# Copies, evictions, projections and the next layer's first work at other steps, and another deal of the down products, in a two-layer attention and feed-forward kernel

## The reference, cut to what matters

```python
# x: (4, 512, 512) float16
xn = _layernorm(x)
q, k, v = xn @ Wq, xn @ Wk, xn @ Wv          # 32 query heads of 16, 8 key heads of 16
attn = softmax((q @ k.T) / sqrt(16))          # per head, 512 x 512
s = (attn @ v) @ Wo
h = silu(x_gate) * x_up                       # x_gate, x_up = fwht(xn * SU_ug) @ W.T, 2048 wide
g = fwht(h * SU_dp) @ W_down.T                # fwht: a Walsh-Hadamard transform
x = x + s * silu(g)
# layer 1: a gated delta-rule attention and a feed-forward with signs of the weights
```

## Time and profile before

| | us |
|---|---|
| median of 3 runs (lowest, highest) | 1400.39 (1399.33, 1401.78) |
| profiled execution, its own time | 1401.55 |
| its span, first to last instruction | 1399.8 |
| first score group to the last one issued | 47.83 to 720.70 |
| layer 1 begins on TensorE | 769.17 |
| PE busy in the span | 1259.5 (90%) |
| DVE, ACT, POOL busy | 1050.2, 787.6, 524.7 |

### The profile page before, as it was taken

The page is one execution under the profiler, slowest core; times in us unless marked ns, Lnnn a source line. Parts: engine busy times, 40 slices in busy tenths (PEclk is TensorE's granted clock), DMA queues, the critical chain, the costliest instruction groups (busy, mean ns, idle before and its releaser), DMA issues. The chain is left out here.

```text
span 1399.8 us, 23475 instructions
## 1 busy us (share of the span) xinstructions
PE 1259.5 (90%) x8738; PEld 643.5 (46%) x8738; DVE 1050.2 (75%) x1823; ACT 787.6 (56%) x1306; POOL 524.7 (37%) x434
## 2 busy tenths in 40 slices
PE   5777977988798897889959999999999999999998
PEld 2332333333333333333324545865477555855475
DVE  6678875778677786778883986868956976968845
ACT  4775765667676685667836752355433652355431
POOL 3589852012211221012301573328431573328431
PEclk9999999999999999999989999999999999999999
DMA  6655643676567765786777024010131024001121
GB/s 238 199 138 95 110 84 72 108 155 136 104 112 156 141 118 96 137 158 119 127 208 283 22 58 90 10 38 27 44 81 38 9 58 91 17 31 40 42 40 46
DMA packets 346561, 135.59 MB, mean 97 GB/s; under 512 B 312176, under 2 KB 333392, under 8 KB 343888
## 3 DMA queue, kind: packets, MB, share of 16 engines
q1 hardware_dynamic: 334032, 132.52, 42.4%
q10 hardware_dynamic: 12416, 1.57, 1.0%
HBM read 44.87 MB, written 17.87 MB: 45 GB/s over the span
## 5 line engine op out<-in xcount | busy, mean ns | idle before, releaser
L1165 PE MATMUL bank<-rows,both 128*128 128x512 f16 x1024 | 250.2, 391 | 38.8 <-DVE th L657 22.4
L944 ACT ACTIVATE probs<-vpair,top_n 128x512 f16<-128x512 f32 x256 | 170.5, 687 | 141.3 <-DVE top_n L638 141.2
L638 DVE TENSOR_REDUCE top_n<-vpair 128x1 f32<-128x512 f32 x256 | 169.3, 682 | 64.5 <-PE bank L1134 64.0
L1179 PE MATMUL bank<-dn,h 128*128 128x512 f16 x768 | 182.6, 386 | 0.0
L1165 PEld LDWEIGHTS bank<-rows,both 128*128 128x128 f16 x1024 | 95.9, 100 | 176.5 <-DVE th L657 36.6
L944 ACT ACTIVATE probs<-bank,top_n 128x512 f16<-128x512 f32 x256 | 164.4, 687 | 0.0
L638 DVE TENSOR_REDUCE top_n<-bank 128x1 f32<-128x512 f32 x256 | 163.3, 678 | 0.0
L454 POOL TENSOR_TENSOR h<-th,h 128x512 f16<-128x512 f32 x61 | 70.5, 1155 | 225.0 <-ACT h L913 225.0
L2246 PE MATMUL bank<-rows,both 128*128 128x512 f16 x512 | 117.3, 380 | 0.0
L1179 PEld LDWEIGHTS bank<-dn,h 128*128 128x128 f16 x768 | 71.3, 99 | 93.7 <-issue 17.8
L2262 PE MATMUL bank<-both,hid 128*128 128x512 f16 x512 | 111.2, 379 | 0.0
(11 more groups left out here) (357 smaller groups left out, 2556.5 us busy)
## 6 DMA issues: line engine op xcount, KB each, us to landing
h<-in_ug SPq DMA_DIRECT2D x8, 1024.0 KB, 6.5
lt_scratch<-big SPq DMA_DIRECT2D x16, 384.0 KB, 2.8
dn<-in_down SPq DMA_DIRECT2D x2, 2048.0 KB, 11.5
x_scratch<-th SPq DMA_DIRECT2D x16, 256.0 KB, 3.1
res<-x_scratch SPq DMA_DIRECT2D x16, 256.0 KB, 4.3
out_x<-res SPq DMA_DIRECT2D x16, 256.0 KB, 2.0
both<-in_w SPq DMA_DIRECT2D x2, 1548.0 KB, 11.4
t_scratch<-tok SPq DMA_DIRECT2D x16, 192.0 KB, 2.1
```

Of the source, the lines that this page charges most:

```text
L638: v.tensor_reduce(top_n[:, i:i + 1], SC_[n % G][:, :], AX.X, ALU.max, negate=True).then_inc(S["max_done"], 1)
L944: a.activation(probs[:, k % TAKEN, j * T:(j + 1) * T], SC_[j][:, :], ACT.Exp, bias=top_n[:, i:i + 1]).then_inc(S["p_ready"], 1)
L1165: mm = pe.matmul(GB[n % 2][:, :], w[:, kt, col:col + P], xnb(b, kt), start=r == 0, stop=r == 2 * KT - 1)
L1179: mm = pe.matmul(bk, h16(ft, r // 2)[:, rows], dn16(ft, r % 2), start=j == 0 and r == 0, stop=j == FT - 1 and r == 2)
```

## The change

Only layer 0's tables and the order inside a step change; no computation does. In the numbering of the kernel before:

- K of the next batch is projected at step 61 instead of 57 (and evicted at 62 instead of 58).
- ScalarE, in a step with a score group: `tanh_down` now stands first, `high_rows` and the copy of a turned x ahead of all four exponentials. Before, `high_rows` stood behind the first exponential, the copy behind the fourth, and `tanh_down` at the end of the step.
- The down products of a round are dealt by `DOWN_MM`, 192 over 32 steps, instead of six a step, and none of them is issued ahead of its step's score group any more. The intervals that also hold `weigh`, a Q projection or an output product get fewer, the others more.
- The output products of the third and fourth tile stand at steps 26 and 34 instead of 28 and 35, and so do `gated`, `residual` and the store.
- In round 4, layer 1's statistics, maxima and scaling stand at step 8 (behind the last score group) instead of 3, the split and the halves two or so steps later, `turn_next` at 21 instead of 19, its copies at 22 instead of 20, and the loads and signs of the raw weights at other steps.

```diff
--- before.py
+++ after.py
@@ -36,20 +36,22 @@
 TOKEN_STEP, DIVIDE_STEP, TURN_BACK = 6, 0, 2
 OT = KT + 1
 FFN_STEP = 32
+DOWN_MM = (8, 6, 6, 7, 7, 4, 4, 8, 7, 6, 6, 7, 7, 6, 6, 8, 7, 6, 6, 6, 5, 2, 2, 8, 7, 4, 4, 7, 7, 6, 6, 6)
+DOWN_AT = tuple(sum(DOWN_MM[:m]) for m in range(FFN_STEP + 1))
 DOWN_END = (8, 16, 24, 32)
-OUT_STEP = (20, 22, 28, 35)
-OUT_LAST = (20, 22, 28, 35)
-NEXT_STEP, EVICT_STEP = 19, 20
+OUT_STEP = (20, 22, 26, 34)
+OUT_LAST = (20, 22, 26, 34)
+NEXT_STEP, EVICT_STEP = 21, 22
 XRES_STEP = (17, 19, 24, 25)
-Q_STEP, V_STEP, K_STEP = 5, 43, 57
+Q_STEP, V_STEP, K_STEP = 5, 43, 61
 TEND = B * BSTEPS + OUT_STEP[-1] + 4
 CHUNKS = (0, 4, 1, 5, 2, 6, 3, 7)
 PREP = -2
 DN_AT = (49, 51, 52, 53, 55, 57, 58, 59, 60, 61, 62, 63, 65, 66, 67, 68)
 DN_PAIR_AT = (16, 18, 19, 22, 23) + tuple(range(25, 41)) + tuple(range(41, 62, 2))
 ABS_AT = tuple(9 + 3 * ft // 4 for ft in range(FT))
-RAW_AT = (11, 12, 13, 21, 23, 24, 25, 26)
-SIGN_AT = (18, 19, 20, 21, 22, 23, 26, 34)
+RAW_AT = (13, 14, 15, 21, 23, 24, 25, 26)
+SIGN_AT = (18, 19, 20, 21, 23, 24, 26, 34)
 LOW_FIRST = 3
 POOL_UNITS = range(5, NU - 2)
 ROW_TOP = 2.0 ** 14
@@ -829,7 +831,7 @@
                     divide(ta // STEPS - 2)
                 if ta % STEPS == TURN_BACK and 0 <= ta // STEPS - 2 < NU and ta // STEPS % 2:
                     to_features(ta // STEPS - 2)
-                if b == B and m == 3:
+                if b == B and m == ATT:
                     next_stats()
                     weight_max(0)
                     next_scale()
@@ -839,13 +841,13 @@
                     scale_down((b - 1) * TT + DOWN_END.index(m))
                 if b and m - 2 in DOWN_END:
                     second_gate((b - 1) * TT + DOWN_END.index(m - 2))
-                if b == B and m == 9:
+                if b == B and m == ATT + 3:
                     next_split()
                     weight_scales()
-                if b == B and m == 12:
+                if b == B and m == ATT + 6:
                     for kt in range(KT):
                         weight_low(kt)
-                if b == B and m == 13:
+                if b == B and m == ATT + 7:
                     column_scales()
                 if b and m - 1 in out_step(b):
                     gated((b - 1) * TT + out_step(b).index(m - 1))
@@ -998,17 +1000,17 @@
                 ta = t - ATT
                 paired = ta % 2 and 0 <= ta // 2 < NU * TT
                 fb, fm = (t - 2) // BSTEPS, (t - 2) % BSTEPS
+                if b and m - 1 in DOWN_END:
+                    tanh_down((b - 1) * TT + DOWN_END.index(m - 1))
                 if b < B and m > FFN_STEP and m % 2:
                     tanh_gate(b, (m - FFN_STEP) // 2)
-                if paired:
-                    exps(G * (ta // 2))
                 if 0 <= fb < B and fm > FFN_STEP and t % 2:
                     high_rows(fb, (fm - FFN_STEP) // 2)
-                if paired:
-                    for j in range(1, G):
-                        exps(G * (ta // 2) + j)
                 if t in TURN_STEP:
                     evict_x(KT + TURN_STEP.index(t))
+                if paired:
+                    for j in range(G):
+                        exps(G * (ta // 2) + j)
                 if 0 <= t - PREP - 2 < NCH * KT:
                     high_half(t - PREP - 2)
                 for ft in range(FT):
@@ -1022,11 +1024,9 @@
                     evict_k(b + 1)
                 if t in DN_AT:
                     high_down(DN_AT.index(t))
-                if b and m - 1 in DOWN_END:
-                    tanh_down((b - 1) * TT + DOWN_END.index(m - 1))
-                if b == B and m == 9:
+                if b == B and m == ATT + 3:
                     weight_high()
-                if b == B and m == 10:
+                if b == B and m == ATT + 4:
                     a.wait_ge(S["const_in"], CONST_END)
                     a.activation(W["negA"], W["negA"], ACT.Exp).then_inc(S["t_negA"], 1)
                 if t - B * BSTEPS in SIGN_AT:
@@ -1184,8 +1184,8 @@
 
                 b, m = t // BSTEPS, t % BSTEPS
                 if b and m < FFN_STEP:
-                    for i in range(first, min(last, 6)):
-                        down_mm((b - 1) * TT + m // 8, 2 * (m % 8) + i // 3, i % 3)
+                    for i in range(DOWN_AT[m], DOWN_AT[m + 1]) if last else ():
+                        down_mm((b - 1) * TT + i // (3 * FT), i // 3 % FT, i % 3)
                 if b < B and m >= FFN_STEP:
                     for r in range(first, last):
                         ffn_mm(b, m - FFN_STEP, r)
@@ -1225,7 +1225,7 @@
             for t in range(TEND):
                 b, m = t // BSTEPS, t % BSTEPS
                 ta = t - ATT
-                ahead = 1 if ta % 4 == 1 else 0
+                ahead = 1 if ta % 4 == 1 and m >= FFN_STEP else 0
                 if t in TURN_STEP:
                     turn_x(KT + TURN_STEP.index(t))
                 ffn(t, 0, ahead)
```

## The result

| | us |
|---|---|
| median of 4 runs (lowest, highest) | 1369.72 (1367.72, 1370.98) |
| the kernel before beside it, same chip | 1401.09 (1399.33, 1405.75) |
| ratio, 95% interval | 0.977 (0.974 to 0.980) |
| profiled execution, its own time (span) | 1370.98 (1369.1) |
| layer 1 begins on TensorE | 740.19 |

A forecast was written before the change was run, and what follows sets the result against it. Layer 0 was taken as bound by a loop of products, maxima and exponentials, no engine full. Terms -17 - 5 + 0.6 - 4 - 1 - 2 = -28.4 from 1400.4 gave 1372 us; own range 1364 to 1380, 8 in 10 1355 to 1387.

The forecast's parts named there:

- `high_rows`: Gate halves: `up_mul` no longer waits for GpSimd's high half, some 18 times 0.23, -4 us; step 1 of rounds, -1.
- the deal: Down products dealt unevenly over layer 0's intervals: cost 0 by itself, hidden under maxima and exponentials.
- K: Step 61 instead of 57: ScalarE's waits for query copies go; -7.3, -6.9, -2.6 in rounds 1, 2, 0, sum -17 us.
- Copies in round 0: Copies of turned x ahead of the exponentials: shorter PE waits for MISC, limited by GpSimd; -5 us, between 0 and -9.
- `tanh_down` first: Step 25, rounds 1 to 3: third tanh waits for the first store, exponentials queue behind; +3.2 at R2.27, +4.1 at R2.29.
- Rival A: The third tanh does not stall at step 25; SP's transposes become the bound at step 33: 1359 us, chance 0.22.
- Output products at 26 and 34: Steps 33 to 37: third tile's store lands before `up_mul` needs it, 13.21 us becomes 9.5, -3.7 a round.
- Sum of both over rounds 1 to 3: Steps 9 to 37, stalls and stores together: +0.4 in rounds 1 and 2, -0.2 in round 3, sum +0.6 us.
- Rival C: 64 gate pairs: `high_rows` delays the exponentials by 0.6 us each, so the kernel is slower: 1411 us, chance 0.05.
- The seam: Layer 0 to layer 1: PE's 13.20 us hole moves later, VectorE's chain ends where it did; -2 us, between -6 and +4.
- Rival B: Only K pays: round 0 held by GpSimd, `up_mul` by its own bank, seam ends on the signs: 1387 us, chance 0.18.
- Rival D: The new order changes nothing, some other chain such as SP's sets the intervals: 1400 us, chance 0.03.

The follow-up runs named there:

- the kernel with an even last tile: Changed kernel, with each round's last-tile down products dealt 5, 6, 6, 6, 6, 6, 6, 6 over steps 24 to 31: 1365.55 us, ratio 0.975.
- the kernels with a cure: Changed kernel with third tanh behind the exponentials (1360.31 us), first store ahead of key copies (1358.43), both (1355.84), or both plus evenly dealt last tile (1355.23).
- both cures: Changed kernel with the third tile's tanh behind the exponentials and the first tile's store ahead of the key copies on SP: 1355.84 us, ratio 0.9675.

## Why the prediction was right, step by step

The total held (1372 against 1369.72; 30.6 us in the profiled execution for a forecast of 28.4), and the largest terms held one by one. That it held so closely is in part luck: `high_rows` gained 5 us more than forecast, while the deal, costed at nothing, lost 2 to 4 us and the copies gave 1 to 2 us less.

*K, forecast -17:* measured -16.7, round by round as forecast (-7.3, -7.1, -2.3 for -7.3, -6.9, -2.6). The reasoning was that nothing else covers the wait, and nothing did.

*Copies in round 0, forecast -5:* 3 to 6, by the medians 3.3 to 4. R0.33 was 5.1 us earlier; the interval at R0.23 grew from 6.01 to 12.09, where GpSimd holds PE as I expected (4.38 us in one wait).

*`tanh_down` first, forecast +3.2 at step 27 and +4.1 at step 29, early gains swallowed:* right in mechanism and size. Counted from step 9 of rounds 1 to 3, step 27 came 3.3, 3.8 and 3.1 us later than before and step 29 4.4, 4.7 and 3.6 (for +4.1, +4.1 and +3.5). The interval at 25 itself grew by more, 4.0, 4.8 and 4.8 us, because the group came 0.7, 1.1 and 1.8 us sooner and SP did not: what was gained ahead of the wait became waiting, as forecast. The cold clock and the missing work at 27 I had at +0.9; measured +1.0, +0.9, +0.6. Behind the hole a product took 0.37 us, in the kernel without one 0.23. The Trainium skill (TensorE: Matmul & The Clock Gate, Part 1: The HAM clock gate) says that the slow clock is the default and that activity releases it; the trace agrees, with these two numbers. But a hole was not always paid twice: behind one of 3.40 us in the kernel with an even last tile the clock stayed up. Rival A (no stall) falls with the 5.66 us wait. What it said of a kernel without the stall came out: 1359 forecast, 1355 to 1360 in the kernels with a cure, and SP's transposes as the bound at step 33, 3.6 us in round 2 with both cures.

*Output products at 26 and 34, forecast -3.7 a round:* 13.21 to 9.62, -3.6. But their worth is not additive: taken out alone they cost 6 us, not 11; the likely reason is that the stall already gives SP the time.

*Sum of both over rounds 1 to 3, forecast +0.6:* +2.0.

*The deal, forecast 0:* not hidden under maxima and exponentials, as I had it, but a loss of 2 to 4 us. It wins 0.76 us at step 5 and loses it in the stall, loses 0.3 us in the mean at step 21, and its 8 and 14 products in intervals 25 and 27 cost up to 2 us a round with the clock. With the stall cured the part at steps 24 to 31 is 0, but by two effects that cancel; whether the rest of the table then pays, no run shows. The loss stands mostly inside the numbers of steps 9 to 37.

*`high_rows`, forecast -5:* -10. The step that failed is the size in "some 18 times 0.23". Six intervals a round over three rounds are the 18, but each gave 0.3 to 0.6 us, 0.4 in the mean, and round 3 had 1.2 more; 0.23 was the mean of the wait of one link, which the bound engine does not pay at that price. Step 1 gave 1.4 for 1. Rival C (`high_rows` delays the exponentials) is the opposite of what was measured; its 1411 should read 1410.

*The seam, forecast -2:* -1.3 to -1.6, and with the hole later and for the last transposes, as said. The reason given, that VectorE's chain ends where it did, is not what the rows show: behind the hole PE is the bound.

Rival B (only K pays) falls too: the K edit alone is 14 us short of the changed kernel. Rival D (nothing changes) falls with the 31 us.

## What to carry to other kernels

Before an instruction is put first on its engine, look for every semaphore it waits on, also one that "had always been there": this one waited 0.24 us where it stood and 5.66 where it went, and took four exponentials and the clock with it. Where one queue (here SP) is without a gap, time won ahead of a wait on it can be lost at the wait, and undoing an edit alone measures less than the edit's interval shows. Taking work out of an interval in which the matrix engine already idles can cost the clock: with two products instead of five or six at step 21 the interval was 0.4 us shorter in a third of the cases and 0.4 to 0.8 us longer in the others. A wait on an engine that others wait for in turn can be worth more than its row says; read the interval of the bound engine with and without it (0.6 us), not the idle time of one link (0.23).

## What the runs showed of the hardware that was not expected

From the issue of the first tile's store to the start of the tanh that waited for it passed 2.7 us in rounds 2 and 3 of the changed kernel and 4.3 in round 1; over all kernels here 2.7 to 4.6. What decides it is open.

The same instructions with the same idle time gave two different intervals at step 21, 6.25 us with a granted clock of 1.00 and 7.11 to 7.52 with 0.77 to 0.84. And a hole of 3.40 us in one round was followed by full clock, one of 2.82 us in another round of the same kernel by 0.50.

Round 0, with the same instructions, took up to 3 us more or less from execution to execution (R0.61: 11.73 or 9.84 us).
